# A block of cross-attention and a feed-forward layer on one core: the sixth context tile split in halves, VectorE making the low halves between its keys, a store and the last batch's tiles put in another order

## The chip, the cores and the metric

The kernel runs on one core of a Trainium2 chip. The metric is the device time of one execution in microseconds (us), lower is better. The core has TensorE (PE; PEld is its weight load), VectorE (DVE), ScalarE (ACT), GpSimd (POOL) and SyncE (SP), which only issues DMAs. All share one SBUF; TensorE writes PSUM, in banks of 512 float32 columns.

## The reference

```python
def _L0_xattn_ref(query, key):              # query 8x100x2048, key = ctx_4096, 8x722x2048
    a = jnp.einsum('bqd,bkd->bqk', query, key)
    e = jax.nn.softmax(a, axis=-1)
    return jnp.einsum('bqk,bkd->bqd', e, key)

x = x + jnp.tanh(g_xattn[0]) * _L0_xattn_ref(_layernorm(x), ctx_4096)
# qweight 2048x1536 int32, each group of three words holding four 6-bit values
w = (unpacked.astype(jnp.float32) - zero_point) * scale
x = x + jnp.tanh(g_ffn[0]) * (jnp.einsum('bsk,nk->bsn', _layernorm(x), w) + bias)
```

All is float32. The scores are not divided by a root, so they are large, and the kernel keeps nearly the whole float32 precision in both attention products.

## The kernel before

**Tiles.** A batch has 100 query rows and 722 context rows; the context lies in SBUF as six tiles of 128, 128, 105, 128, 128 and 105 rows by 2048 columns (`raw[:, b % 2, t, :]`, two batches at a time). Where precision is needed a float32 value is split in a high half (the value copied to the type float32r, which TensorE multiplies in one pass) and a low half (value less high half). A product is then three passes, high by high, high by low, low by high; a float32 matmul without the split takes one instruction that lasts longer.

**Stages of a batch.** `scores(b)` on TensorE turns the context into 32 "keys" (two groups of context rows by 16 chunks of 128 columns: three transposes of `raw` into one of four PSUM banks), ScalarE copies each out as `khi` (L552), VectorE makes `klo` from the bank and `khi` (L912), and three keys later (`AHEAD`) TensorE multiplies: two matmuls by `khi` (L1056) and one by `klo` (L1058). A bank is free again once its `klo` is made. The list `between` (ScalarE) and `hooks` (VectorE) put other work ahead of the key with the number given. `attend(b)` multiplies the probabilities by the context tiles, in the order `ORDER`, into four banks. Tiles 0 to 4 (`HALVED = 5`) go in three passes by `vhi` and `vlo` (L1094), tile 5 as a float32 matmul straight from `raw` (L1105). `vhi` is made by ScalarE (`context_hi`, L563), `vlo` by GpSimd (`context_lo`, L495, 38 of them); both have three buffers (`PAIRS`), taken again when TensorE has used the tile. The last batch halves three tiles only.

**Loop.** Iteration `i` is `scores(i + 1)`, then `attend(i)`, with the transposes of the queries of batch `i + 2` between its tiles. VectorE adds the result of batch `i - 1` to the residual (`residual`, L783, four pieces) before the keys of iteration `i`; TensorE can write the banks again after that. `ln1_norm` and `ln2_norm` are ScalarE's applications of the layer norms, fed by VectorE's statistics and GpSimd's eight small instructions of `rstd`.

**Loads.** SyncE issues in the program's order. It loads a context tile again when its low half is made (`used`), for tile 5 when TensorE has multiplied it (`s_pvt`). At the start it loads the first two batches in 48 pieces of 512 columns.

**The second half.** The rows of all batches after the second norm go to DRAM (`rows_out`) and come back as seven tiles of 128 rows (`load_rows`). VectorE unpacks the weights (`unpack(n)`, L836 to L843, after `load_w(n)`), TensorE transposes them (`weights`, L1131) and the rows (`normed`), and `multiply(nb, m)` runs 32 matmuls of float16 (L1164). The last two attentions are mixed with the first of these transposes. In this stretch SyncE issues, in this order, `rows_out` of batch 6, `load_rows(3)`, `load_w(5)`; and `rows_out` of batch 6 waits for `ln2_norm(6)` on ScalarE.

## Time and profile before

| | |
|---|---|
| time, median of 3 runs (lowest to highest) | 589.73 us (585.59 to 604.38) |
| the profiled execution | 585.18 us, its span 583.3 us |
| PE / PEld busy | 569.0 us (98%) / 409.8 us (70%) |
| DVE / ACT / POOL busy | 358.9 (62%) / 287.7 (49%) / 217.0 us (37%) |
| mean granted clock of TensorE | 0.999 |
| DMA | 113.69 MB, 195 GB/s over the span |

The span is the profiled execution without what lies around it (1.9 us). Instructions of one engine overlap at their ends, so the time of a row is longer than the step to the next one. "Idle before" is how long the engine stood still ahead of an instruction, with what released it. The stages are: start to 41 us (queries and keys of batch 0), seven iterations to about 362 us, the last attention to 390 us, and the feed-forward multiplication to the end.

### The profile page before, as it was taken

How to read it: one execution, taken by the hardware profiler on the slowest of the kernel's cores; microseconds unless marked ns; L12 is line 12 of the kernel's file. 1: busy time of each engine (PE TensorE's matmuls, PEld its weight loads, DVE VectorE, ACT ScalarE, POOL GpSimd, SP SyncE). 2: the span in 40 equal slices, each digit the busy share in tenths (PEclk: the TensorE clock that was granted, in tenths of full speed). 3: DMA queues.
4: the chain of work that ended last, by engine and by line, in shares of the span. 5: the costliest groups of instructions: out<-in, count | busy, mean ns of one | idle time of the engine just before them, and what ended most of it. 6: DMA issues, size and time to landing. Idle time of an engine off the chain costs nothing.

```text
span 583.3 us, 8789 instructions
## 1 busy us (share of the span) xinstructions
PE 569.0 (98%) x3454; PEld 409.8 (70%) x3454; DVE 358.9 (62%) x684; ACT 287.7 (49%) x451; POOL 217.0 (37%) x196
## 2 busy tenths in 40 slices
PE   7979999999999999999999999989999999999997
PEld 6969969968968968978977986555564444444445
DVE  6667717827836836745755764694859764654443
ACT  3756566568567666676675757354232220210000
POOL 3037177169259349439439519711000000000000
PEclk9999999999999999999999999999999999999999
DMA  8999649236947848738848668669756984872311
GB/s 247 296 299 242 193 160 319 66 104 225 228 144 249 225 108 298 224 98 261 265 104 281 193 161 366 225 111 284 233 183 187 252 237 134 194 152 66 89 55 40
DMA packets 44436, 113.69 MB, mean 195 GB/s; under 512 B 21027, under 2 KB 21283, under 8 KB 35779
## 3 DMA queue, kind: packets, MB, share of 16 engines
q1 hardware_dynamic: 27168, 107.71, 60.7%
q10 hardware_dynamic: 16970, 5.42, 5.2%
q8 instruction: 27, 0.44, 0.4%
q14 instruction: 15, 0.11, 0.1%
q0 software_dynamic: 256, 0.00, 0.0%
HBM read 89.26 MB, written 19.66 MB: 187 GB/s over the span
## 4 chain that ended last, share of the span: by engine, by line
PE 79%; DVE 7%; DMA 5%; POOL 3%; SPq 3%; issue 1%; ACT 1%
PE S L1164 18%; PE S L1056 12%; PE T L1010 8%; PE pv L1164 8%; PE S L1058 7%; PE pv L1094 6%; PE S L1094 6%; PE pv L1010 5%; POOL vlo L495 3%; DMA xa<-in_x 3%; DVE xres L783 3%; PE pv L1105 2%; PE S L1105 2%; DMA raw<-in_L_ffn_qweight 2%; SPq L330 2%
## 5 line engine op out<-in xcount | busy, mean ns | idle before, releaser
L495 POOL TENSOR_TENSOR vlo<-raw,vhi 128x2048 fp32r<-128x2048 f32 (+1 forms) x38 | 174.1, 4606 | 50.3 <-ACT vhi L563 50.3
L1056 PE MATMUL S<-khi,qT 128*100 128x362 f32 x512 | 141.3, 357 | 0.0
L1058 PE MATMUL S<-klo,qT 128*100 128x362 f32 x256 | 85.3, 333 | 3.5 <-DVE klo L912 3.0
L912 DVE TENSOR_TENSOR klo<-pv,khi 128x361 fp32r<-128x361 f32 x128 | 65.3, 527 | 23.6 <-ACT khi L552 23.0
L912 DVE TENSOR_TENSOR klo<-T,khi 128x361 fp32r<-128x361 f32 x128 | 65.7, 529 | 21.5 <-ACT khi L552 20.6
L563 ACT ACTIVATE vhi<-raw 128x2048 fp32r<-128x2048 f32 (+1 forms) x38 | 72.0, 1911 | 6.3 <-PE S L1094 6.2
L552 ACT ACTIVATE khi<-T 128x361 fp32r<-128x361 f32 x128 | 58.4, 475 | 33.0 <-PE T L1010 32.8
L1164 PE MATMUL S<-raw 128*128 128x512 f16 x320 | 71.7, 379 | 1.6 <-issue 1.6
L552 ACT ACTIVATE khi<-pv 128x361 fp32r<-128x361 f32 x128 | 58.6, 476 | 29.8 <-PE pv L1010 29.8
L1056 PEld LDWEIGHTS S<-khi,qT 128*100 128x100 f32 x512 | 67.9, 167 | 0.0
L1010 PE MATMUL T<-ident,raw 128*128 128x128 f32 (+1 forms) x416 | 64.0, 268 | 0.4 <-DVE qT L902 0.3
L1010 PE MATMUL pv<-ident,raw 128*128 128x128 f32 (+1 forms) x384 | 59.6, 266 | 0.0
L1164 PEld LDWEIGHTS S<-raw 128*128 128x128 f16 x320 | 31.0, 98 | 37.8 <-ACT raw L537 1.8
L902 DVE TENSOR_TENSOR qT<-T,qT 128x400 fp32r<-128x400 f32 x28 | 14.8, 570 | 69.1 <-ACT qT L543 69.1
L1010 PEld LDWEIGHTS T<-ident,raw 128*128 128x128 f32 (+1 forms) x416 | 53.2, 145 | 5.2 <-issue 0.7
L1010 PEld LDWEIGHTS pv<-ident,raw 128*128 128x128 f32 (+1 forms) x384 | 48.8, 140 | 3.6 <-DVE qT L902 0.7
L1094 PE MATMUL pv<-vhi,ph 128*100 128x512 f32 (+1 forms) x152 | 49.5, 399 | 1.1 <-POOL vlo L495 0.7
L1094 PE MATMUL S<-vhi,ph 128*100 128x512 f32 (+1 forms) x152 | 48.4, 392 | 0.0
L1058 PEld LDWEIGHTS S<-klo,qT 128*100 128x100 f32 x256 | 42.1, 165 | 8.6 <-DVE klo L912 7.9
L474 POOL TENSOR_SCALAR ln<-mr 100x1 f32<-100x1 f32 x16 | 3.7, 229 | 110.1 <-DVE mr L739 109.6
L1164 PE MATMUL pv<-raw 128*128 128x512 f16 x192 | 42.6, 379 | 0.0
L634 ACT ACTIVATE xa<-raw 128x2048 f16<-128x2048 f16 x8 | 15.3, 1911 | 49.0 <-DVE raw L843 49.0
(128 smaller groups left out, 748.6 us busy)
## 6 DMA issues: line engine op xcount, KB each, us to landing
raw<-in_ctx SPq DMA_DIRECT2D x24, 1024.0 KB, 10.4
raw<-in_L_ffn_qweight SPq DMA_DIRECT2D x16, 768.0 KB, 7.7
raw<-in_ctx SPq DMA_DIRECT2D x12, 840.0 KB, 9.0
raw<-in_ctx SPq DMA_DIRECT2D x32, 256.0 KB, 10.2
xres<-in_x SPq DMA_DIRECT2D x8, 800.0 KB
x_scratch<-xres SPq DMA_DIRECT2D x8, 800.0 KB
rows_scratch<-xres SPq DMA_DIRECT2D x8, 800.0 KB
late<-x_scratch SPq DMA_DIRECT2D x24, 256.0 KB, 4.8
```

The lines of the kernel that those rows point to most:

```text
L495: pool.tensor_tensor(vlo[0:r, k, :], raw[0:r, b % 2, t, :], vhi[0:r, k, :].bitcast(F32), ALU.subtract).then_inc(s_vlo, 1)
L552: act.activation(khi[:, (b * 2 * CH + f) % RING, 0:GW], T[k][:, 0:GW], ACT.Copy).then_inc(s_khi, 1)
L563: act.activation(vhi[0:ROWS[t], n % PAIRS, :], raw[0:ROWS[t], b % 2, t, :], ACT.Copy).then_inc(s_vhi, 1)
L634: act.activation(wn[n % 2], unp[n % 2].rearrange("p j g -> p (j g)").bitcast(F16), ACT.Copy, bias=-float(BIAS16)).then_inc(s_wn, 1)
L783: dve.scalar_tensor_tensor(out=piece, in0=pv[n][0:R, :], scalar=soft[0:R, i % 2, 3:4], in1=piece, op0=ALU.mult, op1=ALU.add).then_inc(s_x1, 1)
L912: dve.tensor_tensor(klo[:, slot, 0:GW], T[k][:, 0:GW], khi[:, slot, 0:GW].bitcast(F32), ALU.subtract).then_inc(s_free[k], 1)
L1010: last = pe.transpose(dst(T[k]), src, ident[0:n, 0:n])
L1056: pe.matmul(into[0:R, g, 0:MW], qT[:, h, c, :], khi[:, slot, :], start=(c == 0 and h == 0), stop=False)
L1058: last = pe.matmul(into[0:R, g, 0:MW], qT[:, 0, c, :], klo[:, slot, :], start=False, stop=(c == CH - 1))
L1094: last = pe.matmul(pv[n][0:R, :], ph[0:r, p, t, :], v[0:r, k, n * 512:(n + 1) * 512], start=(first and a == 0), stop=(final and a == 2))
L1105: last = pe.matmul(pv[n][0:R, :], p, raw[0:r, b % 2, t, n * 512:(n + 1) * 512], start=False, stop=final)
L1164: last = pe.matmul(ACC[(j + k) % NA][0:r, cols], xT[m][:, h, c, :], WT[nb % 2][:, c, cols], start=(c == 0 and h == 0), stop=(c == CH - 1 a ...
```

## The change

Six tiles are halved in batches 0 to 6 (`HALVED = 6`), so the float32 tile is gone there, and the order is 0 to 5. Their low halves move from GpSimd to VectorE; GpSimd keeps the three of the last batch. Where tiles 0 to 2 are made between keys, VectorE takes them in pieces of 512 columns at the keys listed in `places`; tiles 3 to 5 come in two halves of 1024 columns each during `attend`. The last batch goes 3, 0, 5, 1, 4, 2 and starts with a float32 tile. ScalarE's `ln1_norm` moves to key 28 (31 in iteration 0), VectorE's statistics move earlier, the fill order of the banks and the weights' transposes follow. `ln2_norm` of batch 6 comes after `weights(3)`. At the start all four pieces of `x[0]` are issued by SyncE, `x[1]` ahead of the last six pieces of context 0, and `queries(1)` stands inside the keys of batch 0. SyncE stores `x1` of batch 6 (the seventh) ahead of the load of `xres`.

```diff
-    HALVED = 5
+    HALVED = 6
-    ORDER = [0, 1, 2, 5, 3, 4]
+    ORDER = [0, 1, 2, 3, 4, 5]
-    LAST_ORDER = [0, 1, 5, 3, 2, 4]
+    LAST_ORDER = [3, 0, 5, 1, 4, 2]
...
-            for c in (0, 2):
+            for c in range(NCH):
                 sp.dma_start(xa[0:R, piece(c)], x[0, :, piece(c)]).then_inc(s_xa0[c], 16)
...
+                        if (b, g, c) == (0, 1, 2):
+                            next_x(1)
...
+            x1_out(LAST - 1)
             next_xres(LAST)
-            x1_out(LAST - 1)
...
+                if i + 2 < B:
+                    between[28 if i else 31] = lambda: ln1_norm(i + 2)
                 keys_hi(i + 1, between)
                 probs(i)
                 exps(i + 1)
-                if i + 2 < B:
-                    ln1_norm(i + 2)
                 context_hi(i, 3)
                 context_hi(i, 4)
-                context_hi(i + 1, 0)
                 if i + 2 < B:
-                    queries(i + 2)
+                    context_hi(i, 5)
+                    queries(i + 2, (0, 1))
+                    context_hi(i + 1, 0)
+                    queries(i + 2, (2, 3))
...
-            ln2_norm(LAST - 1)
             weights(2)
             weights(3)
+            ln2_norm(LAST - 1)
...
+            def context_lo(b, t, part, parts):
+                r, k, cols = ROWS[t], (b * HALVED + t) % PAIRS, slice(part * D // parts, (part + 1) * D // parts)
+                dve.wait_ge(s_vhi, b * HALVED + t + 1)
+                low = dve.tensor_tensor(vlo[0:r, k, cols], raw[0:r, b % 2, t, cols], vhi[0:r, k, cols].bitcast(F32), ALU.subtract)
+                if part == parts - 1:
+                    low.then_inc(s_vlo, 1)
...
                 if i + 2 < B:
-                    hooks = pieces_of(i + 2, 17 if i else 22, 3 if i else 2)
+                    hooks = pieces_of(i + 2, 11 if i else 19, 2)
...
+                lows = [(t, part) for t in range(PAIRS) for part in range(2 if i and not t else 0, 4)]
                 if i == 0:
-                    hooks[3] = lambda: row_max(0)
-                    hooks[13] = first_coef
+                    places = [5, 6, 7, 8, 9, 10, 11, 12, 13, 14, 15, 16]
+                elif i + 2 < B:
+                    places = [5, 7, 9, 19, 21, 23, 25, 27, 29, 30]
+                else:
+                    places = [5, 6, 7, 8, 10, 11, 13, 14, 15, 16]
+                for f, (t, part) in zip(places, lows):
+                    hooks[f] = lambda t=t, part=part: context_lo(i, t, part, 4)
+                if i == 0:
+                    hooks[4] = lambda: row_max(0)
+                    hooks[18] = first_coef
                 keys_lo(i + 1, hooks)
                 probs_lo(i)
                 row_max(i + 1)
                 if i >= 1:
-                    ln2_stats(i - 1)
+                    ln2_stats(i - 1, (0, 1))
+                for half in range(2):
+                    context_lo(i, 3, half, 2)
+                if i >= 1:
+                    ln2_stats(i - 1, (2, 3))
+                for half in range(2):
+                    context_lo(i, 4, half, 2)
                 coef(i + 1)
+                if i + 2 >= B:
+                    rows_lo(0, 0)
+                for half in range(2):
+                    context_lo(i, 5, half, 2)
                 if i + 2 < B:
-                    queries_lo(i + 2)
+                    queries_lo(i + 2, (0, 1))
+                    for part in range(2):
+                        context_lo(i + 1, 0, part, 4)
+                    queries_lo(i + 2, (2, 3))
...
-                    attend(i, {3: lambda: normed(0, (0, 1)), 4: lambda: normed(0, (2, 3)), 5: lambda: probs(LAST)})
-            attend(LAST, {1: lambda: weights(0), 2: lambda: weights(1), 3: lambda: normed(1, (0, 1)),
-                          4: lambda: normed(1, (2, 3)), 5: lambda: weights(2)})
-            weights(3)
+                    attend(i, {2: lambda: normed(0, (0, 1)), 4: lambda: probs(LAST), 5: lambda: normed(0, (2, 3))})
+            attend(LAST, {0: lambda: weights(0), 1: lambda: weights(1), 2: lambda: normed(1, (0, 1)),
+                          3: lambda: normed(1, (2, 3)), 4: lambda: weights(2), 5: lambda: weights(3)})
```

The order on VectorE at the end of the keys of a middle iteration, before (L731 are the statistics of the next `x`, L796 opens `probs_lo`):

```order
L731 BN_STATS stats<-xa 100x6
L739 BN_AGGR mr<-stats 100x2
L912 TENSOR_TENSOR klo<-pv,khi 128x361 x2
L912 TENSOR_TENSOR klo<-T,khi 128x361 x2
L912 TENSOR_TENSOR klo<-pv,khi 128x361
L796 TENSOR_TENSOR ph<-T,ph 128x200
```

The same place in the changed kernel, from key 26 on (L791 is `context_lo`, L917 the keys, L799 opens `probs_lo`):

```order
L917 TENSOR_TENSOR klo<-pv,khi 128x361
L791 TENSOR_TENSOR vlo<-raw,vhi 105x512
L917 TENSOR_TENSOR klo<-pv,khi 128x361
L917 TENSOR_TENSOR klo<-T,khi 128x361
L791 TENSOR_TENSOR vlo<-raw,vhi 105x512
L917 TENSOR_TENSOR klo<-T,khi 128x361
L791 TENSOR_TENSOR vlo<-raw,vhi 105x512
L917 TENSOR_TENSOR klo<-pv,khi 128x361 x2
L799 TENSOR_TENSOR ph<-T,ph 128x200
```

Behind key 28 (the first `klo<-T` shown) two pieces now stand, one ahead of key 29 and one ahead of key 30, where only keys stood before.

The order on ScalarE around the last attention, before (L615 copies turned rows, L579 is `ln2_norm`, L537 copies turned weights):

```order
L537 ACTIVATE raw<-T 128x8x128 x4
L615 ACTIVATE raw<-T 128x512 x4
L579 ACTIVATE xres,rsum<-xres,shift,mr 100x2048
L537 ACTIVATE raw<-T 128x8x128 x4
L615 ACTIVATE raw<-T 128x512 x4
L579 ACTIVATE xres,rsum<-xres,shift,mr 100x2048
```

And in the changed kernel (L607, L571 and L529 in the same roles):

```order
L529 ACTIVATE raw<-T 128x8x128 x4
L607 ACTIVATE raw<-T 128x512 x4
L529 ACTIVATE raw<-T 128x8x128 x4
L571 ACTIVATE xres,rsum<-xres,shift,mr 100x2048
L607 ACTIVATE raw<-T 128x512 x4
L571 ACTIVATE xres,rsum<-xres,shift,mr 100x2048
```

The first `ln2_norm` of the two, that of batch 6, now stands behind the four copies of `weights(2)` and `weights(3)`.

## Rows read from the trace of the kernel before

**Rows 1.** Busy time by stretch, one middle iteration: engine busy (instructions), clock, DMA.
```profile
113.00:158.60 45.60, 45.50 (x285) 37.98 (x284) 27.62 (x56) 30.77 (x51) 27.78 (x23) 1.00 0.58 174
```

**Rows 2.** TensorE's timeline in that iteration: start us, us, instruction, count.
```profile
120.43 0.62 PE L1094 MATMUL pv<-vhi,ph 105*100 105x512 f32 x2
...
123.19 1.88 PE L1105 MATMUL pv<-raw,pT 105*100 105x512 f32 x4
...
126.62 0.85 PE L1010 MATMUL T<-ident,xa 100*128 100x100 f32 x8
...
144.32 0.33 PE L1058 MATMUL S<-klo,qT 128*100 128x362 f32 x1
...
145.30 0.41 PE L1058 MATMUL S<-klo,qT 128*100 128x362 f32 x1
...
157.51 0.33 PE L1058 MATMUL S<-klo,qT 128*100 128x362 f32 x1
...
158.31 0.33 PE L1058 MATMUL S<-klo,qT 128*100 128x362 f32 x1
...
160.49 0.63 PE L1094 MATMUL pv<-vhi,ph 128*100 128x512 f32 x2
```

**Rows 3.** VectorE's timeline there: in brackets the idle time before and its releaser.
```profile
132.13 1.40 DVE L783 SCALAR_TENSOR_TENSOR xres<-pv,soft,xres 100x512 f32<-100x512 f32 x2
...
134.76 0.97 DVE L912 TENSOR_TENSOR klo<-T,khi 128x361 fp32r<-128x361 f32 x2
...
144.71 0.98 DVE L912 TENSOR_TENSOR klo<-T,khi 128x361 fp32r<-128x361 f32 x2 [1.90 <-ACT khi L552]
...
151.41 0.53 DVE L912 TENSOR_TENSOR klo<-pv,khi 128x361 fp32r<-128x361 f32 x1 [0.27 <-ACT khi L552]
...
161.52 2.46 DVE L731 BATCH_NORM_STATS2 stats<-xres 100x6 f32<-100x512 f32 x4
```

**Rows 4.** ScalarE's timeline there: the two long instructions between keys.
```profile
137.28 1.91 ACT L563 ACTIVATE vhi<-raw 105x2048 fp32r<-105x2048 f32 x1
...
142.14 2.09 ACT L579 ACTIVATE xres<-xres,shift,mr 100x2048 f32<-100x2048 f32 x1
```

**Rows 5.** Groups by line and form, VectorE, 448 to 583 us: busy us, mean ns.
```profile
L875 DVE TENSOR_TENSOR late<-late,consts 128x512 f32<-128x512 f32 x18 | 12.5, 692 | 0.6
```

**Rows 6.** GpSimd's timeline: first and last of the eight instructions of `rstd`.
```profile
130.21 0.21 POOL L474 TENSOR_SCALAR ln<-mr 100x1 f32<-100x1 f32 x1
...
132.53 0.24 POOL L488 TENSOR_SCALAR shift<-ln 100x1 f32<-100x1 f32 x1
```

**Rows 7.** VectorE's timeline at the start: start us, us, instruction, idle before.
```profile
31.67 0.69 DVE L731 BATCH_NORM_STATS2 stats<-xa 100x6 f32<-100x512 f32 x1 [3.18 <-DMA xa<-in_x]
...
38.46 1.29 DVE L755 TENSOR_SCALAR xa<-xa,mr 100x2048 f32<-100x2048 f32 x1
```

**Rows 8.** TensorE's timeline in the keys of batch 0.
```profile
32.86 0.41 PE L1058 MATMUL S<-klo,qT 128*100 128x362 f32 x1 [1.89 <-DVE klo L912]
...
40.24 0.41 PE L1058 MATMUL S<-klo,qT 128*100 128x362 f32 x1 [0.85 <-DVE klo L912]
```

**Rows 9.** TensorE's timeline, last two attentions and first multiplications.
```profile
342.73 0.63 PE L1094 MATMUL pv<-vhi,ph 128*100 128x512 f32 x2
...
389.86 2.32 PE L1164 MATMUL S<-raw 128*128 128x512 f16 x10 [1.63 <-issue]
...
403.25 1.13 PE L1131 MATMUL T<-ident,raw 128*128 128x128 f16 x16 [0.45 <-DVE late L815]
```

**Rows 10.** SyncE's timeline: the store of the rows of batch 6.
```profile
382.93 0.30 SPq L318 DMA_DIRECT2D rows_scratch<-xres  x1
```

**Rows 11.** One line, `load_rows`: issue ns min/median/max, first and last start.
```profile
L371 SPq DMA_DIRECT2D xa<-rows_scratch x4: 327/362/3643, 313.2 to 419.7; - x4
```

**Rows 12.** The chain that ended last, in order of time: start us, us.
```profile
387.01 13.50 DMA raw<-in_L_ffn_qweight
```

**Rows 13.** One line, `load_w` (L358): its 16 loads from issue to landing.
```profile
DMA to landing us min/median/max: 5.2/7.7/15.3
```

More of the change, by code:

```diff
@@ L510, in _ @@
             rstd(0, 1)
-            pool.wait_ge(s_q, NCH + 1)
-            for t in range(PAIRS):
-                context_lo(0, t)
             for i in range(B):
@@ L516, in _ @@
                     rstd(0, i + 2)
+                if i >= 1:
+                    rstd(1, i - 1)
                 if i == LAST - 1:
-                    rstd(1, i - 1)
-                for t in range(PAIRS, halved(i)):
-                    context_lo(i, t)
-                if i >= 1 and i != LAST - 1:
-                    rstd(1, i - 1)
-                if i < LAST:
                     for t in range(PAIRS):
-                        context_lo(i + 1, t)
+                        context_lo(t)
                 if i >= 1:
@@ L784, in residual, with ln2_stats @@
                                              op0=ALU.mult, op1=ALU.add).then_inc(s_x1, 1)
-            def ln2_stats(i):
+            def ln2_stats(i, pieces=range(NCH)):
                 dve.wait_ge(s_x1, i * NCH + NCH)
-                for c in range(NCH):
+                for c in pieces:
                     stats_piece(1, i, xres[i % 2], c)
-                mean_and_variance(1, i)
+                if NCH - 1 in pieces:
+                    mean_and_variance(1, i)
+            def context_lo(b, t, part, parts):
[4 more added lines that the diff above has]
+                    low.then_inc(s_vlo, 1)
             def probs_lo(b):
```

61 lines of the change are left out of this document (30 added, 31 removed).

## The prediction

> **What bounds the kernel now.** I read the table of stretches first, then TensorE's timeline of one iteration, then its waits at the start and in the last attention. In a middle iteration TensorE is busy for 45.50 of 45.60 us at clock 1.00, VectorE for 27.62, GpSimd for 27.78 [rows 1]: the kernel is bound by TensorE there, and a change gives time back only as less work on TensorE, or takes some by making it wait. It waits at two ends. In the keys of batch 0 it stands 1.89 and 0.85 us for `klo` [rows 8], because VectorE waits 3.18 us for the load of `x[1]` and then does a 1.29 us centring between keys [rows 7]. From the first matmul of attention 6 (342.73) to the first multiplication (389.86) 47.13 us pass, and later 403.25 is a wait for a bank that ends a chain over the load of a weight tile [rows 9, 12].
>
> **The float32 tile.** Tile 5 takes 126.62 - 123.19 = 3.43 us as float32; tile 2, with the same 105 rows, takes 123.19 - 120.43 = 2.76 us in three passes [rows 2]. The change saves 0.67 us in each of seven attentions; the seventh is counted with the end below, so six: **-4.0 us**.
>
> **VectorE's new work.** No row shows this instruction. The nearest is L875, float32 with both inputs in SBUF, 512 columns, 692 ns [rows 5]. Consecutive instructions overlap: two keys take 0.97 us where one takes 0.53 [rows 3], so a key occupies 0.44 us, 0.09 less than its row, and four statistics take 2.46 us, about 0.59 each [rows 3]. I take 0.60 us for a piece of 512 columns (bounds: 0.59 from the statistics, 0.69 without overlap) and 1.15 us for a half tile of 1024: from 361 columns in 0.53 us to 512 in 0.692, a further 512 cost 0.55. A middle iteration gets 12 pieces' worth for tiles 0 to 2 (10 between keys, 2 in the attention) and six halves: 7.2 + 6.9 = 14 us, for 27.6 + 14 = 41.6 of some 45 us. VectorE is not the bound by its sum; what counts is where each piece stands.
>
> **Between the keys.** TensorE takes a key each 158.31 - 157.51 = 0.80 us [rows 2]. A key with a piece ahead of it takes VectorE 0.44 + 0.60 = 1.04 us, so each such key uses 0.23 us of a lead and each bare one returns 0.37. The lead can be read: `ln2_norm` at key 12 lets ScalarE deliver `khi` late, VectorE idles 1.90 us where 0.27 is usual [rows 3], 1.63 late, and TensorE's step to the next `klo` is 145.30 - 144.32 = 0.98, 0.18 over its pace [rows 2]. So the lead is about 1.45 us. Today each of ScalarE's long instructions falls on keys with nothing behind them. In a middle iteration now:
>
> - Key 6: `vhi` (1.91 us [rows 4]; 0.18 shorter than the norm without its read of the sum, so about 1.36 late) leaves 0.1 of lead; the piece ahead of key 7 costs 0.23. TensorE waits 0.1.
> - Key 12: 0.18 as before; now a statistic (0.59) stands ahead of key 13: 0.2 more. Keys 15, 17 and the pieces at 19 to 27, one key in two, get their 0.23 back.
> - Key 28: `ln1_norm`, the size of `ln2_norm` (2.09 us [rows 4]) but without the read, about 1.55 late: 0.1. Then pieces ahead of keys 29 and 30 with no bare key between. TensorE's second transpose of the probabilities goes into the bank of key 29 and waits for its `klo`, 1.04 us after that of key 28, where it would be there after 0.4: 0.65. Today the last keys run without a wait, 158.31 to 160.49 [rows 2].
>
> That is 1.1 us for each of iterations 2 to 5. Iteration 1 has no norm at key 12: 0.9. Iteration 0 puts `row_max` at key 4 and twelve pieces at keys 5 to 16 without a gap: 13 keys ask 1.1 + 12 x 0.60 + 13 x 0.44 = 14.0 us of VectorE where TensorE takes 10.5: 3.5 late, 1.4 covered, 2.1 waited, and 0.5 for `ln1_norm` at key 31: 2.6. Iteration 6 has ten pieces in keys 5 to 16 and two long instructions: 0.4 up to key 11, 0.2 at 12 and 0.9 for 13 to 16: 1.5. Sum 4.4 + 0.9 + 2.6 + 1.5 = **+9.4 us**. Below this: if every piece found a lead, only the runs of iterations 0 and 6 would be left, about 3; above: at 0.69 a piece, 0.09 more for each key in the runs that have no lead (some 50), 14.
>
> **In the attentions** I cost the rest at nothing. Counting from the attention's first matmul, with 2.76 us a tile, tile 0 is used at 2.8, `vhi` of tile 3 is there at 4.8, its two halves at 7.2, wanted at 8.3; tile 4 is made by 10.9 (two statistics ahead of it) and wanted at 11.7, tile 5 by 13.5 and 15.0; the residual follows at 16.5 to 19.2. Before, the first matmul was at 160.49 - 45.6 = 114.9 [rows 1, 2], so the residual at 132.13 began 17.2 after it, and the keys, at 134.76, 19.9 [rows 3]. The cover is thin: from 4.8 us on VectorE has no idle time, and each us late there is a us of TensorE's. GpSimd loses 35 of its 38 low halves, which nobody else waits for. The context loads of tiles 1 and 2 start some 15 us later than now, with 18 us left before they are needed.
>
> **The start.** `x[1]` is issued six pieces earlier, 1.4 of the 7.5 MB that had landed by 31.67 [rows 7], so it lands near 27 us, when VectorE is just there. The waits of 1.89 and 0.85 go; back come 0.8 for the centring at key 28, right behind the `vhi` of key 27, and up to 0.7 (I take 0.3) for the context pieces that now come later. `queries(1)` inside the keys and the single queue for `x[0]` I put at 0.8 and 0.4, estimates without a row of their own, hence the wide bounds. **-3.0 us**, between -1 and -4.5.
>
> **The end.** TensorE's own work from 342.73 is eight tiles of 2.76, four of 3.43 and some 7.9 of transposes, 43.7 us of the 47.13 [rows 2, 9]; the float32 tile takes 0.7 away and the new order of tiles covers all but 0.4 of the 3.4 waited, so multiplication starts 43.4 us after the first matmul of attention 6, 3.7 sooner. But `ln2_norm(6)` now ends behind `weights(3)`, near 44.2, and the store of the rows of batch 6, which stands on SyncE ahead of `load_rows(3)` and `load_w(5)`, goes from 382.93 (40.2) [rows 10] to 44.4. From that store to the landing of weight tile 5 it took 400.51 - 382.93 = 17.6 us [rows 10, 12], 3.6 of them one issue of L371 whose median is 0.36 [rows 11]. I take 14.3, without that slow issue: landing at 58.7, and 2.7 more through unpacking and `rows_lo` (400.51 to 403.25) to TensorE at 61.4. Before it was 403.25 - 342.73 = 60.5. So the gain in the attention is given back waiting for this load: **+0.9 us**. The bounds: 7.7 us, the usual landing of this line [rows 13], gives 55.7 at TensorE's own pace, -4.8; the full 17.6 gives +4.2. The swap of the store and the `xres` load moves neither far: 0.
>
> **Sum.** -4.0 + 9.4 - 3.0 + 0.9 = +3.3 on 585.18: **588.5 us**. That profiled execution took less than any of the three runs; against the shown median of 589.73 the forecast is no change.
>
> **Rivals.**
> (a) *Faster, by the end.* The load of weight tile 5 lands in its usual 7.7 us [rows 13], since the queue is empty when it is issued. For: the 13.50 us were behind a store and a slow issue. Against: both stand there again. 588.5 - 0.9 - 4.8 = 583 us.
> (b) *Faster, by the keys.* The pieces cost only what the unbroken runs make, +3 instead of +9.4. It is decided by the lead at key 28: with 2.3 us or more there, nothing is waited. For: the lead is read from one place. Against: that place is exact to 0.1. 588.5 - 6.4 = 582; with (a) 577.
> (c) *Slower: VectorE late in the attention.* GpSimd's `rstd`, 2.5 us from 130.21 to 132.77 with some 1.9 busy [rows 6], now runs beside low halves. If each instruction of the two engines holds the other up, the low halves of tiles 4 and 5, the queries and the residual are late by up to 1.9 us; half of that, with 0.2 of cover, is 0.8 in seven iterations, 5.6, and with the end's bound (+3.3 more) 588.5 + 8.9 = 597. It decides once VectorE is over 0.3 us late at the queries. No row of before has such a pair, since a key reads one input from PSUM.
> (d) *The change doesn't do what it says*: the sixth tile might still be waited for longer than it saves; that is (c).
>
> The Trainium skill, "SBUF — State Buffer", section "Who interferes with whom", speaks for (c): a VectorE instruction with two inputs in SBUF and a GpSimd instruction that reads SBUF exclude each other for a whole instruction. By that rule the sum would be that of (c) without the end's bound, about 594; by the row L875, when GpSimd was idle, it is 588.5. No run here shows it yet.
>
> **Numbers.** Forecast (585 to 593 around it) 0.45, (a) 0.18, (b) with or without (a) 0.17, (c) 0.20. The range 577 to 598 leaves out the far halves of (b) and (c), some 0.15. Over 2% (about what a measurement of this kernel can tell from none) is below 578 or above 601: faster 0.10, the low part of (b); slower 0.06, the high part of (c); within 2% 0.84.
>
> **What would show it.** In the changed profile: no L1105 rows in batches 0 to 6; L791 rows of about 690 ns (half tiles near 1,220); TensorE waiting for `klo` or at the transposes of `E` by 0.5 to 0.8 us at the end of each iteration's keys, and about 2 us in iteration 0; an iteration of 45.7 to 46.2 us where it was 45.5; first keys of batch 1 some 3 us earlier; the store of rows 6 about 44 us after attention 6 begins, and TensorE standing still ahead of `normed(3)` or `weights(4)` for 3 to 6 us. The forecast is wrong if an iteration takes under 45 us (then (b)), if the residual starts over 17.5 us after the first matmul (then (c)), or if the first multiplications run without a wait (then (a)).

## The result and the profile after

The changed kernel takes 597.26 us (median of 4, 595.27 to 606.61) where the kernel before takes 588.84 (median of 4, 585.59 to 604.38): ratio 1.014, 95% interval 1.0091 to 1.0189. It is slower by 8.4 us, within 2%, where the prediction had 588.5 against its 585.18. The time lies in the range; the loss is more than twice the +3.3 us forecast. In the profiled executions it is larger still, 596.71 for 585.18, spans 594.0 and 583.3. Medians, here and below, are over all executions, and ratios leave out those in the slower of two states (604.38 and 606.61 here), so the two can differ a little.

First the page of the changed kernel: busy time by engine, the chain that ended last by engine, then three groups (busy us, mean ns | idle before).

```profile
PE 577.4 (97%) x3482; PEld 414.1 (70%) x3482; DVE 447.9 (75%) x817; ACT 299.9 (50%) x458; POOL 85.6 (14%) x161
...
PE 64%; DVE 18%; ACT 7%; DMA 7%; SPq 2%; issue 2%
...
L1084 PE MATMUL S<-klo,qT 128*100 128x362 f32 x256 | 88.1, 344 | 2.6 <-DVE klo L917 1.9
L791 DVE TENSOR_TENSOR vlo<-raw,vhi 128x512 fp32r<-128x512 f32 (+3 forms) x126 | 105.9, 858 | 18.9 <-ACT vhi L555 18.9
...
L472 POOL TENSOR_SCALAR ln<-mr 100x1 f32<-100x1 f32 x16 | 8.7, 544 | 225.8 <-DVE mr L733 225.7
```

VectorE now spends 106 us on low halves, for 42 tiles, of which GpSimd made 35 before. To see where 10.7 us of span came from, I read the same marks on TensorE's timeline in both traces: the use of key 0 of batch 1, the first matmul of each attention, the first multiplication and the transposes of `weights(4)`, as in [rows 2, 9].

| stretch | before | after | difference | predicted |
|---|---|---|---|---|
| start to key 0 of batch 1 | 44.85 | 43.34 | -1.5 | -3.0 |
| to attention 0 (iteration 0) | 24.80 | 27.97 | +3.2 | +2.6 |
| iteration 1 | 45.30 | 45.57 | +0.3 | +0.2 |
| iterations 2 to 5, each | 45.55 | 46.16 | +0.6 (x4) | +0.4 (x4) |
| iteration 6, to attention 6 | 45.57 | 47.50 | +1.9 | +0.8 |
| attention 6 to `weights(4)` | 60.52 | 63.21 | +2.7 | +0.9 |
| `weights(4)` to the end | 180.05 | 181.75 | +1.7 | 0 |

Every middle iteration splits alike. The attention, from its first matmul to the use of key 0, takes 19.81 us where it took 20.39; the keys, from there to the next attention, take 26.35 where they took 25.16. TensorE's timeline at the end of one iteration's keys, and below it the row that follows 158.31 of [rows 2] in the kernel before:

```profile
205.47 0.33 PE L1084 MATMUL S<-klo,qT 128*100 128x362 f32 x1
...
206.35 0.41 PE L1084 MATMUL S<-klo,qT 128*100 128x362 f32 x1
206.60 0.43 PE L1036 MATMUL T<-ident,E 100*128 100x100 f32 x3
207.40 0.48 PE L1036 MATMUL T<-ident,E 100*128 100x100 f32 x3 [0.37 <-DVE klo L917]
...
208.06 0.33 PE L1084 MATMUL S<-klo,qT 128*100 128x362 f32 x1
```
```profile
159.34 0.33 PE L1058 MATMUL S<-klo,qT 128*100 128x362 f32 x1
```

The second transpose of the probabilities waits for the `klo` of key 29. The step between the last two rows of `klo` shown is 206.35 to 208.06, 1.71 us, where the same place before took 1.03 (158.31 to 159.34): 0.68 us more, the wait that the prediction put at 0.65.

The end, on four timelines of the changed kernel: TensorE, ScalarE, SyncE, VectorE (start us, us, instruction, idle before).

```profile
405.58 1.23 PE L1036 MATMUL T<-ident,xa 128*128 128x128 f32 x8 [2.13 <-DMA xa<-rows_scratch]
406.65 3.45 PE L1190 MATMUL S<-raw 128*128 128x512 f16 x8
412.25 1.13 PE L1157 MATMUL T<-ident,raw 128*128 128x128 f16 x16 [2.16 <-DVE late L820]
```
```profile
391.46 2.10 ACT L571 ACTIVATE xres<-xres,shift,mr 100x2048 f32<-100x2048 f32 x1
```
```profile
393.67 0.30 SPq L315 DMA_DIRECT2D rows_scratch<-xres  x1
394.07 0.32 SPq L369 DMA_DIRECT2D xa<-rows_scratch  x1
394.43 1.30 SPq L356 DMA_DIRECT2D raw<-in_L_ffn_qweight  x1
```
```profile
409.59 0.50 DVE L841 TENSOR_SCALAR raw<-raw 128x512 uint16<-128x512 uint16 x1 [8.23 <-DMA raw<-in_L_ffn_qweight]
```

`ln2_norm(6)` begins at 391.46, the store goes out at 393.67, weight tile 5 is issued at 394.43 and is there at 409.59, 15.2 us later; behind it TensorE reaches `weights(4)`. The eight matmuls at 406.65 take 3.45 us where eight take 1.89 at full clock (e1, at 406.77). The table of stretches of the changed kernel shows it (the third number from the right is the granted clock):

```profile
400.00:405.00 5.00, 3.45 (x16) 1.37 (x14) 1.29 (x2) 2.81 (x4) 0.77 (x4) 1.00 1.10 160
405.00:410.00 5.00, 4.42 (x16) 2.06 (x16) 0.41 (x1) 1.08 (x2) 0.65 (x1) 0.68 0.66 169
410.00:415.00 5.00, 2.84 (x23) 1.64 (x23) 2.70 (x7) 1.94 (x2) 0.00 (x0) 0.84 1.43 277
415.00:420.00 5.00, 5.00 (x24) 2.95 (x23) 2.11 (x3) 1.08 (x2) 0.00 (x0) 0.79 0.61 123
```

After the waits TensorE is granted the lower of its two levels (1.2 for 2.4 GHz) for parts of 15 us; before, these stretches were at 1.00.

### The profile page after: what moved, and what is told of

It reads as the page before. It is cut to its first block, busy times and chain, and to the rows that moved or that the text cites. A ratio compares the mean times of both kernels' runs of the same rounds, so it can differ in the third digit from the quotient of the medians.

```text
span 594.0 us, 8953 instructions
## 1 busy us (share of the span) xinstructions
PE 577.4 (97%) x3482; PEld 414.1 (70%) x3482; DVE 447.9 (75%) x817; ACT 299.9 (50%) x458; POOL 85.6 (14%) x161
## 4 chain that ended last, share of the span: by engine, by line
PE 64%; DVE 18%; ACT 7%; DMA 7%; SPq 2%; issue 2%
PE S L1190 17%; PE S L1082 10%; PE pv L1190 8%; DVE vlo L791 8%; PE T L1036 7%; PE S L1084 6%; PE pv L1036 4%; DMA raw<-in_L_ffn_qweight 4%; PE S L1120 3%; PE pv L1120 3%; DMA raw<-in_ctx 3%; DVE xres L777 3%; ACT vhi L555 3%; ACT xa L559 2%; DVE klo L917 2%
## 5 line engine op out<-in xcount | busy, mean ns | idle before, releaser
L791 DVE TENSOR_TENSOR vlo<-raw,vhi 128x512 fp32r<-128x512 f32 (+3 forms) x126 | 105.9, 858 | 18.9 <-ACT vhi L555 18.9
L555 ACT ACTIVATE vhi<-raw 128x2048 fp32r<-128x2048 f32 (+1 forms) x45 | 86.1, 1916 | 15.7 <-PE S L1120 15.7
L1084 PE MATMUL S<-klo,qT 128*100 128x362 f32 x256 | 88.1, 344 | 2.6 <-DVE klo L917 1.9
L917 DVE TENSOR_TENSOR klo<-T,khi 128x361 fp32r<-128x361 f32 x128 | 66.2, 526 | 13.5 <-ACT khi L544 13.4
L917 DVE TENSOR_TENSOR klo<-pv,khi 128x361 fp32r<-128x361 f32 x128 | 65.7, 526 | 12.8 <-ACT khi L544 12.7
L1190 PE MATMUL S<-raw 128*128 128x512 f16 x320 | 74.6, 390 | 0.0
L1120 PE MATMUL pv<-vhi,ph 128*100 128x512 f32 (+1 forms) x180 | 58.5, 399 | 0.0
L1120 PE MATMUL S<-vhi,ph 128*100 128x512 f32 (+1 forms) x180 | 57.4, 393 | 0.0
L892 DVE TENSOR_TENSOR late<-S,consts 128x512 f32<-128x512 f32 (+2 forms) x19 | 12.8, 674 | 42.9 <-PE S L1190 42.9
L472 POOL TENSOR_SCALAR ln<-mr 100x1 f32<-100x1 f32 x16 | 8.7, 544 | 225.8 <-DVE mr L733 225.7
```

Of the source, the lines that this page charges most:

```text
L555: act.activation(vhi[0:ROWS[t], n % PAIRS, :], raw[0:ROWS[t], b % 2, t, :], ACT.Copy).then_inc(s_vhi, 1)
L791: low = dve.tensor_tensor(vlo[0:r, k, cols], raw[0:r, b % 2, t, cols], vhi[0:r, k, cols].bitcast(F32), ALU.subtract)
L892: dve.tensor_tensor(o[0:r, part], ACC[(j + h) % NA][0:r, part], scB[0:r, cols], ALU.mult).then_inc(s_mul, 1)
L917: dve.tensor_tensor(klo[:, slot, 0:GW], T[k][:, 0:GW], khi[:, slot, 0:GW].bitcast(F32), ALU.subtract).then_inc(s_free[k], 1)
L1084: last = pe.matmul(into[0:R, g, 0:MW], qT[:, 0, c, :], klo[:, slot, :], start=False, stop=(c == CH - 1))
L1120: last = pe.matmul(pv[n][0:R, :], ph[0:r, p, t, :], v[0:r, k, n * 512:(n + 1) * 512], start=(first and a == 0), stop=(final and a == 2))
```

## The experiments

Two theories stood against each other. The first: the loss is the sum of stalls at named places, in the keys (pieces and norms ahead of keys) and in the end (one norm's place on ScalarE). Against it: the end and the start are bound by their transfers whatever the order, and (c), that low halves on VectorE and GpSimd's work hold each other up. Each run is given with its median, its ratio to the kernel before, and its profile's marks in this table (us; "it. 2-5" is one iteration, "a6" the first matmul of attention 6).

| run | median | ratio (95%) | key 0, b. 1 | it. 0 | it. 2-5 | it. 6 | a6 to `weights(4)` | then to end |
|---|---|---|---|---|---|---|---|---|
| e1 | 591.94 | 1.0041 (1.0004-1.0079) | 41.39 | 27.95 | 46.17 | 46.87 | 61.93 | 180.0 |
| e2 | 598.18 | 1.0121 (1.0011-1.023) | 45.09 | 27.96 | 45.81 | 46.67 | 62.57 | 182.2 |
| e3 | 593.93 | 1.0129 (1.0012-1.0247) | 41.47 | 25.42 | 45.32 | 44.92 | 63.16 | 188.7 |
| e4 | 599.11 | 1.0178 (1.0123-1.0232) | 48.12 | 27.96 | 46.17 | 46.50 | 62.89 | 180.8 |
| e5 | 597.51 | 1.0176 (1.0122-1.0229) | 50.04 | 24.81 | 45.54 | 45.59 | 68.11 | 181.8 |
| e6 | 582.31 | 0.9878 (0.9832-0.9924) | 42.39 | 25.43 | 45.10 | 44.93 | 56.57 | 180.3 |
| e7 | 596.41 | (too scattered) | 47.27 | 24.89 | 45.96 | 45.66 | 63.33 | 182.9 |
| e8 | 592.24 | 1.0074 (1.0037-1.0111) | 42.65 | 27.97 | 46.20 | 46.79 | 56.41 | 183.0 |
| e9 | 580.69 | 0.9886 (0.9843-0.993) | 44.79 | 25.43 | 45.07 | 44.88 | 56.45 | 180.1 |
| e10 | 582.39 | 0.9881 (0.9834-0.9928) | 42.32 | 25.40 | 45.12 | 44.98 | 56.45 | 190.0 |
| e11 | 585.93 | 0.9967 (0.9928-1.0006) | 44.89 | 24.81 | 45.56 | 45.56 | 59.88 | 180.0 |
| e12 | 582.92 | 0.9915 (0.9874-0.9956) | 48.12 | 25.43 | 45.10 | 44.96 | 57.10 | 180.1 |

### The end: e1, e5, e8

e1, the norm back ahead of the weights:

```diff
+            ln2_norm(LAST - 1)
             weights(2)
             weights(3)
-            ln2_norm(LAST - 1)
```

> The changed kernel, with ScalarE's ln2_norm of batch 6 (LAST - 1) ahead of weights(2) and weights(3) again. My theory is that most of what the last part lost (weights(4) 63.2 us after the first matmul of attention 6, where it was 60.5) comes from this one place in ScalarE's order: GpSimd has the factors at 383.3 us, the norm begins only at 391.5, and the store of these rows and the two loads queued behind it wait for it. Theory: the store is issued near 385.5 instead of 393.7, weight tile 5 is issued near 386.5 and lands 7 to 15 us later, weights(4) comes 54 to 59 us after the first matmul of attention 6, the dip of TensorE's clock after 404 us goes, and the kernel takes 587 to 592 us (5 to 10 less than the changed one). Rival: the landing is set by the queue's own slow issues and by the loads of rows and x1 that stand ahead or beside; then weight tile 5 still lands near 405 to 409 and no more than 2 us come back, 595 to 597.

The ratio falls from 1.014 to 1.0041, intervals apart: this one place in ScalarE's order is worth some 5.8 us by the ratios (0.99% of 588.8). The profiles show less of it in the end: 1.3 us up to `weights(4)` and 1.7 behind; 2.0 more stand at the start and 0.6 in iteration 6, which the edit does not touch. And the theory is missed in part. SyncE's store and loads go out where it had them, counted from attention 6 (383.04, 383.43, 383.79), and yet TensorE waits once more, at another place:

```profile
399.52 1.50 PE L1036 MATMUL T<-ident,raw 128*128 128x128 f32 x8 [3.45 <-DVE raw L820]
400.81 5.17 PE L1190 MATMUL S<-raw 128*128 128x512 f16 x16
```

The chain behind this wait leads to the load of weight tile 4 (13.91 us from 377.55). VectorE waits for that load in `unpack(RT)`, and the residual of batch 7 and the low parts of the rows are queued behind it. The 16 matmuls that follow take 5.17 us, at the lower clock, where the same 16 took 3.62 in the changed kernel. e5 makes the opposite edit, on the kernel before:

```diff
-            ln2_norm(LAST - 1)
             weights(2)
             weights(3)
+            ln2_norm(LAST - 1)
```

> The kernel before, with one edit: ScalarE's ln2_norm of batch 6 behind weights(2) and weights(3), where the change puts it. Theory (the place of this norm sets the store of rows 6 and the two loads behind it): the store moves from 40.2 us after the first matmul of attention 6 to about 49, weight tile 5 lands later by the same, and weights(4) comes 65 to 69 us after that matmul instead of 60.5; with some loss of TensorE's clock after the wait the kernel takes 594 to 599 us. Rival: the transfers set it (the same megabytes have to pass whatever the order) and weights(4) stays within 2 us of 60.5, 588 to 592.

`weights(4)` comes 68.1 us after a6, 7.6 later than before, 1.7 more are lost behind it, and the kernel is 1.76% slower: the theory. This edit alone costs the kernel before as much as the whole change does. (The profile's key 0 of batch 1 at 50.04 is not the edit's: the start of e5 is that of the kernel before.) SyncE's and TensorE's timelines of e5:

```profile
397.02 0.30 SPq L318 DMA_DIRECT2D rows_scratch<-xres  x1
397.41 0.32 SPq L371 DMA_DIRECT2D xa<-rows_scratch  x1
397.78 1.31 SPq L358 DMA_DIRECT2D raw<-in_L_ffn_qweight  x1
```
```profile
408.97 1.23 PE L1010 MATMUL T<-ident,xa 128*128 128x128 f32 x8 [3.68 <-DMA xa<-rows_scratch]
...
416.00 1.16 PE L1131 MATMUL T<-ident,raw 128*128 128x128 f16 x16 [2.48 <-DVE late L815]
```

The store goes out at a6 + 49.1 (40.2 before [rows 10]). e8 keeps e1's edit and takes VectorE's unpacking out of the way:

```diff
-            unpack(RT)
             residual(LAST)
             ln2_stats(LAST)
             rows_lo(2, 0)
             rows_lo(2, 1)
-            unpack(RT + 1)
+            unpack(RT)
             rows_lo(3, 0)
+            unpack(RT + 1)
             rows_lo(3, 1)
```

> The run with ln2_norm of batch 6 ahead of weights(2), and in addition VectorE's unpacking of weight tile 4 behind the low parts of row tile 2, and that of weight tile 5 behind the first half of row tile 3: VectorE no longer waits for a weight tile's load with work behind it that does not need the tile. Theory: TensorE's 3.45 us wait there and the lower clock behind it go, weights(4) comes 57 to 59 us after the first matmul of attention 6 (61.9 without this edit), and the kernel takes 586 to 589 us. Rival: the loads set the pace whatever waits for them; TensorE stops at the next place that needs one (weights(4) itself, or weights(5)), and no more than 1 us is gained, 591 to 593.

`weights(4)` moves to a6 + 56.4, a little ahead of the theory's place, and no stretch there is at the lower clock; but the median stays at that of e1 (592.24 for 591.94), because what lies behind takes 2.9 us more: half a miss. The chain of waits of e8 tells why:

```profile
400.18 1.32 DVE raw L845 x3
401.51 0.21 DVE raw L848
...
401.74 12.47 DMA raw<-in_L_ffn_qweight
...
416.14 0.61 DVE raw L820
...
416.89 1.13 PE T L1157 x16
```

The load of weight tile 6 can go only once tile 4 is unpacked, so unpacking late made it late, and TensorE stands 2.78 us for it, ahead of 416.89.

### The keys: e2, e3, e7

e2 only moves pieces off the last keys:

```diff
-                    places = [5, 7, 9, 19, 21, 23, 25, 27, 29, 30]
+                    places = [1, 3, 5, 7, 9, 19, 21, 23, 25, 27]
```

> The changed kernel, with the ten pieces of VectorE's low halves in the middle iterations (1 to 5) at keys 1, 3, 5, 7, 9, 19, 21, 23, 25, 27 instead of 5, 7, 9, 19, ..., 27, 29, 30: the last keys are bare, all else is as it was. The step of the prediction was that the pieces at 29 and 30 hold TensorE up by 0.65 us in each iteration, at the second transpose of the probabilities. Theory: an iteration takes 45.4 to 45.6 us instead of 46.15, five of them give back 3 us, 594 us. Rival: VectorE is late out of the attention by now (it is the chain there), so pieces at keys 1 and 3 cost what those at 29 and 30 did: an iteration stays at 46.0 to 46.3, 596 to 598 us.

The wait at the transposes is gone (TensorE's rows of e2, step 1.12 for 1.71):

```profile
207.65 0.41 PE L1084 MATMUL S<-klo,qT 128*100 128x362 f32 x1
207.90 0.69 PE L1036 MATMUL T<-ident,E 100*128 100x100 f32 x6
...
208.77 0.33 PE L1084 MATMUL S<-klo,qT 128*100 128x362 f32 x1
```

0.59 comes back there, but an iteration gets only 0.36 shorter: 0.2 is lost behind the pieces that moved ahead (the step from key 0 to key 1 is 1.04 where it was 0.89). That lies between theory and rival; the median shows nothing.

e3 gives the low halves of tiles 0 to 2 back to GpSimd and keeps those of tiles 3 to 5 on VectorE, so that no piece stands between keys (the second hunk is GpSimd's):

```diff
-                lows = [(t, part) for t in range(PAIRS) for part in range(2 if i and not t else 0, 4)]
+                lows = []
...
-                if i == LAST - 1:
+                if i < LAST:
                     for t in range(PAIRS):
-                        context_lo(t)
+                        context_lo(i + 1, t)
```

> The changed kernel, with the low halves of context tiles 0 to 2 made by GpSimd in every batch, as before the change, and those of tiles 3 to 5 by VectorE in the attention, as after it: no piece stands between keys, iteration 0 included. It prices all pieces at once. Theory (the pieces cost what the table of stalls says): an iteration takes 44.9 us (45.54 less 0.67 for the float32 tile) where it takes 46.15, five of them 6 us; iteration 0 gets 2.6 back and iteration 6 1.9, so attention 6 begins near 338.5 and the kernel takes 585 to 588 us. Rival: GpSimd's 4.7 us low halves and VectorE's instructions with two inputs in SBUF hold each other up (in the changed kernel three unpacking instructions beside such a low half took 5.73 us where they take 1.33 alone): tile 0's low half of the next batch falls beside the halves of tiles 4 and 5, the residual comes 2 to 4 us late in each attention, and an iteration takes 46 to 48 us, 594 to 604 us.

An iteration takes 45.32 us, iteration 0 25.4 and iteration 6 44.9; attention 6 begins at 337.93 (349.04 in the changed kernel, 1.9 of that from the start). The attention stays at 19.8: nothing of the rival. One iteration of e3, by engine:

```profile
157.02:202.35 45.33, 45.28 (x287) 38.48 (x287) 34.19 (x63) 32.32 (x51) 21.99 (x21) 1.00 0.73 202
```

So the pieces cost 0.84 in each middle iteration, 2.5 in iteration 0 and, with the wait below, 2.6 in iteration 6. What is left above the 44.9 expected, 0.4, is the statistic ahead of key 13 (0.23: the steps to keys 13 and 14 are 1.03 and 0.89 where they were 0.89 and 0.80) and the norm at key 28 (0.16: 0.88 and 1.11 for 0.80 and 1.03). The whole time misses, 593.9 for 585 to 588: a6 to `weights(4)` stayed at 63.2, and behind 480 us TensorE stood 5.8 us for a transposed weight tile.

e7 is e3 with ScalarE's norm where it was before:

```diff
-                if i + 2 < B:
-                    between[28 if i else 31] = lambda: ln1_norm(i + 2)
...
                 exps(i + 1)
+                if i + 2 < B:
+                    ln1_norm(i + 2)
```

> The run with GpSimd's low halves for tiles 0 to 2 (iterations of 45.3 us: keys 25.55, attention 19.8), with ScalarE's ln1_norm behind the exponentials again instead of at key 28. It prices the place of the norm. Theory: the keys lose the 0.4 us that the norm costs at key 28 (25.1 us), and the attention has 1 us of slack for tiles 3 to 5, so an iteration takes 44.9 to 45.0 us. Rival: the norm makes the vhi of tiles 3 to 5 late by 1.2 us, TensorE waits for a low half, and an iteration stays at 45.3 to 46 us. The end of this kernel is that of the changed one, so its whole time says little: 588 to 595.

The rival: the keys take 25.4 us (25.55 in e3), but the attention 20.5 (19.76). ScalarE's timeline of e7:

```profile
165.36 2.09 ACT L562 ACTIVATE xa<-xa,shift,mr 100x2048 f32<-100x2048 f32 x1
167.35 3.70 ACT L558 ACTIVATE vhi<-raw 128x2048 fp32r<-128x2048 f32 x2
```

The first `vhi` of the attention is 1.1 us late (4.05 us after the first matmul, 2.96 in e3). VectorE's halves of tile 3 are late by as much and all its work behind them, down to the residual (by 0.7), and TensorE's gain of 0.6 in the attention is gone. The theory had the price of the norm at key 28 too high: it is 0.16 us in the keys, not 0.4, and its place saves 0.7 in the attention.

### The start: e4, e11, e9, e10

e4 puts the load of `x[1]` in the changed kernel behind the context pieces again; e11 puts it ahead in the kernel before:

```diff
                     for c in range(NCH):
+                        if (b, g, c) == (0, 1, 2):
+                            next_x(1)
...
             context_pieces(0)
-            next_x(1)
```

> The changed kernel, with the load of x[1] behind all context pieces of batch 0 again; x[0] in one queue and the inner place of queries(1) stay. Theory: the 1.5 us that the start gained (first keys of batch 1 used at 43.34 instead of 44.85) come from x[1] landing earlier, so they are lost again and the centring at key 28 makes it worse: first keys of batch 1 at 45 to 47 us, 599 to 600 us. Rival: the start is bound by the context pieces as a whole, which now land one place earlier: within 0.7 us of the changed kernel, 596 to 598.

> The kernel before, with one edit: the load of x[1] two pieces of columns ahead of the end of batch 0's context pieces, where the change puts it. The prediction gave the start 3.0 us; the changed kernel's profile shows 1.5 (first keys of batch 1 used at 43.34 for 44.85), but other profiles of the same program text at the start gave 41.4 to 47.3. Theory: the place of x[1] is worth 1.5 to 3 us: VectorE's wait for it (3.2 us before, 7.8 in another run) falls under 2 us, the first keys of batch 1 are used at 41.5 to 43.5 us, and the kernel takes 585.5 to 587.5. Rival: the 9.6 MB of the start bound it whatever the order, and the context pieces are waited for instead: 588 to 590 us, first keys at 44 to 46.

e4's keys of batch 1 begin at 48.1, later even than its theory; 599.11 against the changed kernel's 597.26 is the theory's sign, but no more than the scatter. In e11 the theory fails: its 585.93 us lies in the theory's range, but the kernel before, run beside it, took 586.61, the interval of the ratio includes 1, and the first keys of batch 1 are at 44.89, where they were at 44.85. The waits of TensorE from 8 to 56 us in e11:

```profile
PE T L1011 <- DMA raw<-in_ctx: 1.9, 1, 1.9
PE T L1011 <- DVE xa L756: 1.5, 1, 1.5
PE S L1059 <- DVE klo L913: 1.1, 2, 0.8
```

The 1.89 us for `klo` [rows 8] is now 1.9 us for context pieces: one load takes the place of the other. In the changed kernel, whose VectorE wants `x[1]` two keys sooner (key 20 for 22), the late place gave 48.1 (one profile), which is between the two starts of the kernel before (44.85, and 50.04 as e5), so no cost is shown; in the kernel before, the gain of the early place is between nothing and 4 us by the interval.

e9 (`x[1]` two places further ahead) and e10 (`x[0]` in two queues: ScalarE issues the other two pieces) are e6, below, with one edit each:

```diff
-                        if (b, g, c) == (0, 1, 2):
+                        if (b, g, c) == (0, 1, 0):
```
```diff
-            for c in range(NCH):
+            for c in (0, 2):
                 sp.dma_start(xa[0:R, piece(c)], x[0, :, piece(c)]).then_inc(s_xa0[c], 16)
```

> The fastest kernel so far (GpSimd's low halves for tiles 0 to 2, the early norm, the late unpacking), with the load of x[1] two pieces of columns further ahead: in front of the whole second group of context pieces of batch 0. In the profiles so far the first keys of batch 1 were used at 41.4 to 47.3 us wherever x[1] stood two pieces from the end, at 44.9 and 50.0 in the kernel before, and each time it was VectorE's wait for x[1] (0.7 to 7.8 us) that went with the late ones. Theory: that wait is gone, the first keys of batch 1 are used at 41 to 43 us in the profile, and the median is 0 to 2 us lower, because the bad cases go: 580 to 582.5 us. Rival: the context pieces that are pushed back by the 0.8 MB of x[1] are late instead (TensorE waits for them in the keys of batch 0 by 1 to 2 us more): 582 to 585.

> The fastest kernel so far, with two of the four pieces of x[0] issued by ScalarE again, as before the change (x[1] stays two pieces from the end). The prediction charged the single queue with 0.4 us. In the profiles the first queries began at 9.11 us with two queues and at 9.09 with one. Theory: no difference, first queries at 9.0 to 9.2 us, 581 to 584 us. Rival: two queues bring the first queries forward by 0.4 us or more and the context pieces with them, 580 to 582.

Both measure as e6. e10's theory holds, the first queries begin at 9.03. e9's profile has no wait for `x[1]` to speak of (0.3 us), yet its keys of batch 1 begin at 44.79; the stretches of e9, then those of e6, show the reason:

```profile
8.00:12.00 4.00, 2.67 (x16) 2.67 (x17) 3.47 (x8) 1.38 (x3) 2.42 (x8) 0.64 1.02 304
12.00:16.00 4.00, 4.00 (x21) 3.89 (x20) 3.35 (x7) 2.53 (x6) 0.00 (x0) 0.50 1.05 295
```
```profile
8.00:12.00 4.00, 3.25 (x26) 2.57 (x27) 3.96 (x10) 2.65 (x7) 2.42 (x8) 1.00 1.03 312
12.00:16.00 4.00, 4.00 (x30) 3.63 (x30) 3.09 (x7) 2.46 (x6) 0.00 (x0) 1.00 1.06 314
```

In e9 the clock was at its lower level from about 9 to 16 us, beside a stop of 2.2 us for the first queries (1.1 in e6); from 12 to 16 us TensorE gets through 21 instructions in place of 30, and the mark comes 2.4 us later than in e6. The stop alone does not explain it: the kernel before stood 2.18 us at the same place and stayed at 1.00.

### Everything that paid: e6, e12

e6 is the changed kernel with e3's low halves, e1's norm, e8's unpacking, and in iterations 1 to 5 the statistics at keys 14 to 20 and the norm at 26:

```diff
-                    between[28 if i else 31] = lambda: ln1_norm(i + 2)
+                    between[26 if i else 31] = lambda: ln1_norm(i + 2)
...
-                    hooks = pieces_of(i + 2, 11 if i else 19, 2)
+                    hooks = pieces_of(i + 2, 14 if i else 19, 2)
```

> The changed kernel with GpSimd making the low halves of tiles 0 to 2 again, ln2_norm of batch 6 ahead of weights(2), VectorE's unpacking of weight tiles 4 and 5 behind the low parts of the rows that do not need them, the statistics of x at keys 14 to 20 and ln1_norm at key 26 in iterations 1 to 5 (where they stood at 11 to 17 and at 28). Theory: what the change loses lies in the keys and in the order of the end, what it gains (0.6 us in each attention, 3.5 us in the last) is real. Then an iteration takes 44.9 to 45.1 us, attention 6 begins at 336 to 338.5, weights(4) comes 56 to 59 us after it and the kernel takes 575 to 582 us, faster than both. Rival: the end is bound by its transfers, which were issued at the same times after attention 6 began in all kernels so far; TensorE then stands at another place and loses clock, the last part gives nothing back, and the kernel takes 584 to 590.

582.31 us: 1.2% faster than the kernel before, 2.5% faster than the changed one, and the profiled execution at 576.64 is inside the theory's range (its median just above). TensorE has no stop of over 1 us from 10 us to the end; the stretches of e6 from 380 us:

```profile
380.00:390.00 10.00, 10.00 (x55) 6.02 (x54) 7.84 (x14) 2.68 (x5) 2.63 (x9) 1.00 0.61 207
390.00:400.00 10.00, 10.00 (x66) 6.11 (x65) 6.58 (x15) 6.24 (x8) 0.86 (x2) 1.00 0.89 271
```

The rival (the transfers bind whatever the order) is refuted for this part: the same bytes pass, and TensorE is busy throughout at clock 1.00. One thing stays open. The load of weight tile 6 goes out at a6 + 53.9 as in e8, but is there at most 9.95 us later (391.90, used at 401.85) where e8's took 12.47, and no run shows which difference between the two kernels does that.

e12 tried to spare e6 the late load of tile 6 seen in e8, with e9's place of `x[1]`:

```diff
             residual(LAST)
+            unpack(RT)
             ln2_stats(LAST)
             rows_lo(2, 0)
             rows_lo(2, 1)
-            unpack(RT)
```

> The fastest kernel so far with x[1] ahead of the second group of context pieces, and the unpacking of weight tile 4 right behind the residual of batch 6 instead of behind the low parts of row tile 2; tile 5 stays behind the first half of row tile 3. In the run with the norm and the unpacking alone the late unpacking of tile 4 held the load of tile 6 back to 401.7, which came 12.5 us later, and TensorE stood 2.8 us for it; the fastest kernel did not show that wait in its profile. Theory: the load of tile 6 goes out 4 to 5 us sooner after the start of attention 6, no wait appears, and the time is that of the fastest or a little lower, 579 to 582 us. Rival: the low parts of row tile 2 come 2.3 us later, TensorE waits 1 to 2 us for them in the first multiplications and its clock falls: 582 to 586.

No better, 582.92. `weights(4)` comes 0.5 us later than in e6 and nothing behind it gets shorter; at the start its profile has what e9's rival said, TensorE idle for 3.98 us at 26.77, waiting for context pieces.

## Why the prediction was off

The profiles differ by 10.7 us of span where 3.3 were forecast. Of the 7.4 between them the end has 3.5, the start 1.5, iterations 0 to 5 have 1.3 and iteration 6 has 1.1.

**Right, place by place.** The attention gains 0.58 us (0.67 said); the keys of a middle iteration lose 1.19 (1.1 said), at the places named (steps of 0.94 at key 7, 0.97 and 1.03 at keys 12 and 13, where 0.80 is the pace, and 1.71 for 1.03 at the transposes of `E`); a piece takes 0.68 us and steps 0.60; the store of rows 6 comes at a6 + 44.6 (44.4 said); TensorE stands 2.1 us ahead of `normed(3)` and 2.2 ahead of `weights(4)`. Multiplication starts at a6 + 43.62 (43.4 said). The residual starts 16.6 us after the first matmul (179.64, 163.04), under the 17.5 that would have spoken for (c).

**The end, +0.9 said, +2.7 and +1.7 measured: the largest part of the miss.** The term took 14.3 us from the store to the landing, "without that slow issue". The slow issue did not come (0.32 us at 394.07), but the load itself took 15.2 us for 13.5, so it was 15.9 (393.67 to 409.59), and that makes nearly all of `weights(4)` at a6 + 63.2 for 61.4. The other step is one left out: TensorE's clock. The prediction counted 3 to 6 us of standing and nothing behind it, but the profile then shows 0.68, 0.84 and 0.79 from 405 to 420 us. What of this lies ahead of `weights(4)` (eight matmuls in 3.45 us) is inside the wait. What lies behind fits the +1.7: 0.21 of the last 5 us and up to 0.8 us of the stretch before them, 1.1 to 1.9 us as an estimate from these clocks. By the ratios the place of the norm is worth more than the 3.5: e1 gives back 5.8, and e5 costs the kernel before some 10 (9.3 in its profile).

**The start, -3.0 said, -1.5 measured.** The terms given add up to -2.84, with both estimates as gains. The wrong step is "the waits of 1.89 and 0.85 go": in the changed kernel's profile TensorE still waits 1.0 us for `klo` (3.0 before), and 0.9 for context pieces (0.3 said). e11 shows that moving `x[1]` alone buys nothing that can be measured: the pieces of context that it passes are waited for instead (1.9 us). What the changed kernel gained there (41.4 to 47.3 us over the seven profiles with that start, 43.34 in its own) is no larger than what this mark moves from one execution to the next, so what the transposes of `queries(1)` inside the keys are worth stays open. The 0.4 us for the single queue was nothing (e10).

**Iteration 6, +0.8 said, +1.9 measured.** The run of pieces cost what was said. On top came a wait that was not seen: `load_w(1)` waits for the low half of tile 2, now made at key 16, so weight tile 1 arrives late and VectorE stands with keys queued behind the unpacking. TensorE's step there is 1.94 us for 0.81, the whole 1.1 beyond the forecast (in e4, where VectorE stands 0.88 us, the step is 0.95 and the iteration 46.50); in e3, with GpSimd's low halves, there is none. VectorE's and TensorE's timelines of the changed kernel:

```profile
342.48 0.50 DVE L841 TENSOR_SCALAR raw<-raw 128x512 uint16<-128x512 uint16 x1 [1.87 <-DMA raw<-in_L_ffn_qweight]
```
```profile
343.47 0.41 PE L1084 MATMUL S<-klo,qT 128*100 128x362 f32 x1 [0.98 <-DVE klo L917]
```

A buffer is free only when its reader has run; moving the reader later moves the load. The prediction applied this to the context loads of tiles 1 and 2 and forgot the weight tile that takes the same place.

**Iterations 0 to 5** lost 5.9 us for 4.6: iteration 0 3.2 for 2.6, and iterations 2 to 5 0.2 each beyond the forecast, half of it in the attention.

**Rival (c)** had the nearest time (597), by luck: its mechanism, VectorE late in the attention, did not occur. GpSimd's `rstd` in the changed kernel, the first two and the last of eight instructions, and VectorE's halves beside them:

```profile
171.88 1.06 POOL L472 TENSOR_SCALAR ln<-mr 100x1 f32<-100x1 f32 x1 [17.96 <-DVE mr L733]
173.02 1.41 POOL L474 TENSOR_TENSOR ln<-ln,half 100x1 f32<-100x1 f32 x1
...
177.56 1.28 POOL L486 TENSOR_SCALAR shift<-ln 100x1 f32<-100x1 f32 x1
```
```profile
171.71 2.29 DVE L791 TENSOR_TENSOR vlo<-raw,vhi 128x1024 fp32r<-128x1024 f32 x2
...
174.24 2.35 DVE L791 TENSOR_TENSOR vlo<-raw,vhi 105x1024 fp32r<-105x1024 f32 x2
```

The eight instructions take 7.0 us where they took 2.6 [rows 6]; a pair of halves takes 2.29 and 2.35 beside them and 2.36 at 167.94, alone. GpSimd waits, VectorE does not, and nothing hangs on `rstd` here. The Trainium skill, "SBUF — State Buffer", section "Who interferes with whom", has the two exclude each other for whole instructions, and says that the order of issue decides which one waits. The trace agrees: the first of GpSimd's eight begins 0.17 us behind a half of VectorE's and takes 1.06 us, about what is left of that half. What the prediction's "half of that" lacked is this order: VectorE's halves stand back to back, so it was the engine off the path that paid. That no row of before had such a pair was also wrong: VectorE's timeline of the kernel before has it in another form, three unpacking instructions beside GpSimd's low half and three alone.

```profile
367.69 5.73 DVE L840 TENSOR_SCALAR raw<-raw 128x512 uint16<-128x512 uint16 x3
...
384.39 1.34 DVE L840 TENSOR_SCALAR raw<-raw 128x512 uint16<-128x512 uint16 x3
```

Beside a long GpSimd instruction (three low halves in 13.98 us from 358.24, 4.66 each, no longer than usual) it is VectorE that pays.

## What to carry to other kernels

Where a chain of store, load, unpacking and transpose feeds the engine that bounds the kernel, cost a moved instruction by what is queued behind it on every engine and queue down to the load, and look for the next load that will be waited for: three edits each moved a wait to another place (e1, e8, e11), and only e6 and its variants e9 and e12, which have e3's low halves too, show no stop of over 1 us behind the start. A stop of that engine costs more than its length when its clock falls after it. And work between the beats of a pipeline is free only where the engine has a lead; the short last beats, with another consumer of the same banks behind them, are the worst place for it.

## What was not expected of the hardware

- The start and the stretch behind 480 us differ from one execution to the next by more than most edits: the same start gave key 0 of batch 1 at 41.4 to 47.3 us, the kernel before 44.85 and, as e5, 50.04. In e3 TensorE stood 5.8 us for a transposed weight tile near 495 us, and e10 lost 7.7 us near 490: a load of `x1` took 24.03 us (465.03 to 489.06) in a stretch where the DMA engines were fully taken (share 1.0 to 1.5) at 87 to 240 GB/s. A median over several executions is needed for any single edit of 1 to 3 us; e2, e9 and e10 stay undecided by it.
- The lower clock came with stops of about 2 us and more (near 9, 32, 400 and 410 us in various runs), but not with all: behind e8's stop of 2.78 us at 416.89 and behind that of 2.18 us at 9.11 in the kernel before the stretch had 1.00.
